# A graph network's node pass: the layer norm of the sum behind the convolution moves from VectorE to ScalarE

## The reference, cut to what matters

```python
def _layernorm(x, axis=-1, eps=1e-05):
    m = jnp.mean(x, axis=axis, keepdims=True)
    v = jnp.var(x, axis=axis, keepdims=True)
    return (x - m) / jnp.sqrt(v + eps)

h = jnp.maximum(_layernorm(x), 0.0)
x = x + _L0_gnn_ref(h, ...)    # five attention layers: h @ W, edge messages, relu
h = jnp.maximum(_layernorm(x), 0.0)
x = x + _L1_gnn_ref(h, ...)    # a * (gelu(messages) @ Wa + ba) + (1 - a) * h
h = jnp.maximum(_layernorm(x), 0.0)
x = x + _L2_gnn_ref(h, ...)    # graph convolution: gelu(norm-weighted sum of h @ W, + b)
h = jnp.maximum(_layernorm(x), 0.0)
x = x + _L3_gnn_ref(h, ...)    # out = messages + h @ W[0] + bias
```

## Time and profile before

| | |
|---|---|
| median of 3 runs | 5247.03 us (5243.42 to 5260.6) |
| profiled execution, its own time | 5250.73 us |
| its span | 5249.0 us |
| TensorE clock granted, mean | 0.882 of full speed |
| busy share PE / DVE / ACT / POOL | 81% / 77% / 63% / 61% |
| node pass, within the span | about 140 to 1567 us |

### The profile page before, as it was taken

The page is one execution under the profiler, slowest core; times in us unless marked ns, Lnnn a source line. Parts: engine busy times, 40 slices in busy tenths (PEclk is TensorE's granted clock), DMA queues, the critical chain, the costliest instruction groups (busy, mean ns, idle before and its releaser), DMA issues. The chain is left out here.

```text
span 5249.0 us, 101811 instructions
## 1 busy us (share of the span) xinstructions
PE 4269.4 (81%) x28013; PEld 3696.3 (70%) x28013; DVE 4034.0 (77%) x14947; ACT 3328.7 (63%) x9065; POOL 3228.0 (61%) x2905
## 2 busy tenths in 40 slices
PE   4899999999976978969969959877895868879575
PEld 4777777778866867858858848644775857757475
DVE  5799999999986767767757767687566968859765
ACT  2777777777755857847847848644774547768400
POOL 2888888877777727637457367222752247666277
PEclk6999999999988989989989979955997989989755
DMA  3999997666645646636636546488773759857332
GB/s 91 186 221 221 221 220 221 220 221 207 212 155 127 144 86 132 135 77 142 128 89 141 113 102 148 100 246 239 163 144 85 198 158 246 242 125 134 72 94 85
DMA packets 1107279, 825.55 MB, mean 157 GB/s; under 512 B 209510, under 2 KB 1068202, under 8 KB 1106396
## 3 DMA queue, kind: packets, MB, share of 16 engines
q1 hardware_dynamic: 1026800, 690.47, 50.7%
q0 software_dynamic: 77040, 128.08, 12.7%
q10 hardware_dynamic: 2880, 0.50, 0.1%
HBM read 374.78 MB, written 448.11 MB: 157 GB/s over the span
## 5 line engine op out<-in xcount | busy, mean ns | idle before, releaser
L806 POOL DMA_INDIRECT gat_G<-table,k_src_row x980 | 1072.8, 1095 | 316.5 <-issue 282.2
L1599 ACT ACTIVATE gat_Gw<-gat_G,gat_al 128x128 f32<-128x128 f32 x1960 | 618.5, 394 | 88.9 <-DVE gat_al L1424 88.9
L1455 DVE SCALAR_TENSOR_TENSOR gat_Gw<-gat_own,gat_al,gat_Gw 128x128 f32<-128x128 f32 x1960 | 554.7, 343 | 69.2 <-ACT gat_Gw L1599 69.0
L1716 PE MATMUL gat_psG<-gat_ends_at,gat_Gw 128*128 128x128 f32 x3920 | 538.1, 282 | 43.7 <-DVE gat_Gw L1455 43.6
L1744 PE MATMUL gat_psZ<-gat_aggT,t_gat_wh 128*128 128x256 f32 x1960 | 526.3, 392 | 15.3 <-ACT gat_hT L1625 14.9
L1716 PEld LDWEIGHTS gat_psG<-gat_ends_at,gat_Gw 128*128 128x128 f32 x3920 | 493.4, 197 | 54.9 <-DVE gat_Gw L1455 51.9
L635 PEld LDWEIGHTS nodes_psR<-t_ident_v,nodes_hTl 128*128 128x128 f32 x3168 | 431.7, 192 | 105.5 <-issue 1.8
L635 PE MATMUL nodes_psR<-t_ident_v,nodes_hTl 128*128 128x132 f32 x3168 | 446.1, 278 | 0.0
L479 POOL TENSOR_TENSOR nodes_rstd<-nodes_var,k_half 128x14 f32<-128x14 f32 x140 | 365.7, 2612 | 127.0 <-DVE nodes_var L546 127.0
L1625 ACT ACTIVATE gat_hT<-gat_psZ,t_gat_bias 128x256 f32<-128x256 f32 x490 | 231.1, 472 | 267.4 <-PE gat_psZ L1745 261.9
L1744 PEld LDWEIGHTS gat_psZ<-gat_aggT,t_gat_wh 128*128 128x128 f32 x1960 | 340.1, 194 | 56.1 <-ACT gat_aggT L1606 17.2
(11 more groups left out here) (672 smaller groups left out, 12721.8 us busy)
## 6 DMA issues: line engine op xcount, KB each, us to landing
table<-nodes_rows SPq DMA_DIRECT2D x660, 198.0 KB
table<-nodes_n SPq DMA_DIRECT2D x396, 192.0 KB
gat_own<-table SPq DMA_DIRECT2D x490, 132.0 KB
table<-gat_rows SPq DMA_DIRECT2D x392, 132.0 KB
nodes_x<-in_x SPq DMA_DIRECT2D x132, 192.0 KB
out<-nodes_x_out SPq DMA_DIRECT2D x132, 192.0 KB
gat_G<-table,k_src_row POOLq DMA_INDIRECT x980
hgt_q<-enter_q SPq DMA_DIRECT2D x98, 144.0 KB, 2.2
```

Of the source, the lines that this page charges most:

```text
L806: eng.indirect_dma_start(to, None, table, bass.IndirectOffsetOnAxis(ap=index, axis=0)).then_inc(sem, 16)
L1455: ins = eng.scalar_tensor_tensor(Gw[:, i % RS, t, h, :], own[:, i % RO, t, 0:D], al[:, g % 2, 1, a:a + 1], Gw[:, i % RS, t, h, :], ALU.mul ...
L1599: ins = eng.activation(Gw[:, i % RS, t, h, :], G[:, i % RG, t, 0:D], ACT.Copy, scale=al[:, g % 2, 0, a:a + 1])
L1716: mm = eng.matmul(o[:, h * P:(h + 1) * P], Gw[:, i % RS, t, h, :], ends_at[:, i % RE, t, :], start=True, stop=True)
```

## The change

VectorE no longer does n3. ScalarE does it, in three activations of the form Identity(rstd x input + shift), directly behind the newest block's norm and ahead of `hT6`. `shift`, which until now was only formed in steps with a newest block (k < 132), is formed in all steps that have a norm (k < 140). ScalarE signals `nC`; who waits for `nC` is as before (PE's turning of n3, SP's store, VectorE's L613). The wait for the ring of stores (`st7`) moves along with the norm.

```diff
@@ vector
                     if k < N + 8:
                         eng.wait_ge(s.small, n_small)
                         eng.wait_ge(s.pow, k + 1)
-                    if is_block(k):
+                    if k < N + 8:
                         eng.tensor_tensor(shift[:, k % 4, :], negmean[:, k % 4, :], rstd[:, k % 4, :], ALU.mult).then_inc(s.shift, 1)
...
-                    b = k - 8
-                    if is_block(b):
-                        if b >= RB:
-                            eng.wait_ge(st7[b % RB], 16 * (b // RB))
-                        normed(k, n3[:, b % RB, :, :], xs[:, b % SB, :, :], at_3, T, s.nC)
@@ scalar, behind the newest block's norm
                         ins.then_inc(s.nA, 1)
+                    d = k - 8
+                    if is_block(d):
+                        eng.wait_ge(s.shift, k + 1)
+                        if d >= RB:
+                            eng.wait_ge(st7[d % RB], 16 * (d // RB))
+                        for t in range(T):
+                            ins = eng.activation(n3[:, d % RB, t, :], xs[:, d % SB, t, :], ACT.Identity,
+                                                 bias=shift[:, k % 4, at_3 + t:at_3 + t + 1],
+                                                 scale=rstd[:, k % 4, at_3 + t:at_3 + t + 1])
+                        ins.then_inc(s.nC, 1)
                     c = k - 5
```

## The result

The changed kernel takes 5381.7 us in the median (5380.5 to 5388.3, 4 runs), the kernel before 5245.2 us (5239.1 to 5260.6, 4 runs). The ratio is 1.0263 with a 95% interval of 1.0248 to 1.0277: slower by 136.5 us, where 144 us were forecast (5391 us, range 5360 to 5450).

A forecast was written before the change was run, and what follows sets the result against it. One ScalarE-TensorE loop was taken as the bound: 142.6 us for the activations plus 1.5 us for the last steps gave 144 us, 5395 us on the profiled execution, 5391 us as median; range 5360 to 5450 us.

The forecast's parts named there:

- The size: ScalarE's half of the loop: three activations add 1.15 us in each of 124 steps, 142.6 us.
- the last steps: Last eight steps, k = 132 to 139: added shifts and the norm by ScalarE cost 1.5 us in all.
- One side sum: VectorE kept waiting at L613 could meet GpSimd's 1.02 us sum every step: 34 x 0.1 = 3 us more without slots.
- Nothing off for VectorE: Three instructions removed from VectorE, 0.77 us a step, take nothing off because no pace-setting loop goes through them.
- Rival 1: VectorE is the bound and the step shrinks by 0.77 us in 132 steps: -102 us, 5145 us; chance 0.08.
- Rival 4: Less VectorE work lets GpSimd's power, 2.6 us a step, start earlier; nothing by itself, counted to rival 2.
- rival 2: ScalarE's idle time, over 2 us a step, hides the added work and the time stays 5247 us; chance 0.06.
- The new wait closes no slower loop: VectorE's wait at L613 for n3: its loop takes 10.1 us, under the new step of 12.1 with slots.
- rival 3: VectorE's new wait at L613 closes a slower loop with stalls: 108 or 170 us more, 5499 or 5561 us; chance 0.10.
- a sign that I had named against me: Forecast wrong if steps grow by much more than 1.15 us with TensorE waiting for n2 or ScalarE for n1.
- n1's way to ScalarE: From L613 to n1's end VectorE works 7.2 us, then ScalarE 2.9 us: 10.1 us, under 12.1.
- 17 us for a clock of 0.98: TensorE's clock at 0.98 would lengthen its half by 0.14 us, 17 us over 124 steps; taken as 0, kept for the range.

The follow-up runs named there:

- experiment 1: Kernel before, VectorE keeping n3, plus three scratch activations of n3's form on ScalarE directly behind the newest block's norm: 5381.6 us, ratio 1.0271.
- experiment 2: Kernel before plus the same kind of three scratch activations, at the end of ScalarE's step: 5252.9 us beside 5244.4, ratio 1.0017.
- experiment 6: Kernel before with ScalarE's copy of the fourth layer's rows moved to the end of its step: 5249.3 beside 5259.5 us, ratio 0.9986.
- experiment 3: Changed kernel with VectorE's sum with the bias one step later, so VectorE no longer waits for n3: 5382.7 us, ratio 1.0269.
- experiment 4: Kernel before with VectorE doing n3 for one tile of three from the fourth block on: 5250.7 beside 5259.5 us, ratio 0.9988.
- experiment 9: Experiment 8 with GpSimd's sum xb put directly ahead of its power: 5221.5 us beside 5250.7, ratio 0.9949 against the kernel before.
- experiment 7: Changed kernel with n3's activations at the end of ScalarE's step and what follows n3 one step later: 5280.9 us, ratio 1.0036 against the kernel before.
- experiment 11: Kernel before with the fourth layer's row copy at the end of ScalarE's step and GpSimd's sum ahead of its power: 5248.2 us, ratio 0.9990.
- experiment 8: Experiment 7 with ScalarE's copy of the fourth layer's rows also at the end of its step: 5263.3 us, ratio 1.0009 against the kernel before.

## Why the prediction was right

*The loop.* The step was said to be ScalarE's half plus TensorE's half, closing through L754 and L793 with slots and through L797 and L709 without. After the change the ScalarE half has grown from 4.01 to 5.16 us and the TensorE half has stayed (6.94 and 6.93). Experiments 1 and 2 show it apart from everything else: the same instructions cost all or nearly nothing by place. Without slots the account was too simple. There TensorE's only wait in the step of the earlier trace rows was for L773:

```profile
1304.35 0.55 PE L627 MATMUL nodes_psA<-k_ident,nodes_rows 128*128 128x128 f32 x3 [0.19 <-ACT nodes_rows L773]
```

From there it worked on past L709; that path was as long as the one through L797. Work added ahead of both counts in full, as n3 did, but work taken off between them gives nothing, as experiment 6 shows.

*The size.* 1.15 us by L773's rows; the new activations take 1.16 and 1.15. 90 steps were to give 103.5 us and gave 99.9, since the first of them were uneven before already (two of 13.4 us by ScalarE's copies, at a clock of 0.87); 34 steps 39.1 and gave 39.9; the last steps 1.5 and gave 2.7. Sum 144.1 forecast, 140.0 in the pass with the 2.5 us less at the start, 136.5 in the medians. One side sum was off with no effect: 9.7 + 1.02 us is 0.02 us over 10.7 and not 0.1, so 1 us more without slots by the page's rule and not 3.

*Nothing off for VectorE.* Right: experiments 3 and 4. VectorE's share of 95 to 97% was in part stalls that moved nobody; it dropped by 17 points with slots and 21 without, and the kernel got slower. Rival 1 (5145 us) fails by experiment 4. The Trainium skill, "Perfetto Trace Analysis", section "Identifying the Most-Contended Engine", takes the engine with the highest occupancy as the one to optimize first, which in the steps with slots was VectorE; here the measurement decides against it. Rival 4, relief, gave nothing for this change, as forecast, but it is what experiment 9 lives on. And rival 2, that idle time hides the work, would have been right for another place, as experiment 2 shows, and not for the one chosen.

*The new wait closes no slower loop.* Right for the time (rival 3 fails: experiment 3). But half of a sign that I had named against me did show: TensorE waits for n2, 24.7 us in 45 times, against 3.9 us in 5 before. I had worked out n1's way to ScalarE and not n2's to TensorE. It is harmless because turning n2 comes in the ScalarE half: in the step above TensorE waited 0.58 us at 606.51 and then not at all for the newest block's norm, in the next it waited 0.38 us for that norm (620.13) and not for n2. It has time to give until `hT0` comes. In experiment 7, where ScalarE's half is shorter, the same kind of lateness came onto the path and cost 0.9 us a step without slots. I also took the stall to fall into VectorE's wait, at no cost; it fell on L608 or L538 and cost nothing because VectorE's round had room.

*The rule of the page.* That the loser of the shared port waits in full ("SBUF — State Buffer" of the Trainium skill, section "SBUF: two separate sides") agrees with the rows in this: VectorE's operation lasts until the sum is over (L538 at 610.95 to 611.67, the sum to 611.63) and is stretched by 0.5 to 1.4 us. But that section also says that whichever of the two starts first has the port pair. At 621.26 VectorE's operation had started 0.45 us ahead of the sum's recorded start, and it was VectorE's that took 1.89 us. By the recorded starts the measurement differs from the page there; in that step, in the one of the earlier trace rows and in experiment 7's, GpSimd was issuing an indirect DMA when the operation began and went on to the sum at once, and no run tells the two apart.

*The clock.* I had kept 17 us for a clock of 0.98 because TensorE would be less busy. It was 1.00 in both stretches after the change. So the reason I gave was wrong in its direction: TensorE was less busy, and the clock held. The 17 and 21 steps with a fall in experiments 6 and 11 all hold a wait of TensorE for n2 of 0.9 us or more, and the changed kernel's longest wait for n2 from 225 to 1225 us is 0.8 us. But such waits also go by without a fall (3 in experiment 6, 9 in experiment 11, and those of 1.1 us in experiment 7's steps without slots, at a clock of 1.00), so what decides it is not settled.

## What to carry to other kernels

Before moving work between engines, follow one step's loop: which engine waits for which, and where it closes. Work moved into the part of another engine's queue that lies on the loop costs its whole duration, even if that engine has more idle time than the work needs and the one relieved is 97% busy; behind the point where the loop leaves that engine it is nearly free (9 us in place of 136 here). A busy share can be stalls: compare an operation's mean with its shortest time (815 ns and 183 ns for L538 on 14 columns, 225 to 1225 us). And when a place is found, look again at what the shorter loop meets next; here it was another engine's stall (experiment 7), cured by moving GpSimd's sum into a wait of VectorE (experiment 9), and with slots GpSimd's round (experiments 6 and 11).

## What the runs showed of the hardware that I had not expected

- Three activations on 128 x 128 float32 with bias and scale by partition take 1.15 to 1.16 us of the queue, Identity as Relu, out of `x`, `xs` or a scratch tile.
- A VectorE operation can be stretched by a GpSimd sum of 1.0 us by more than that sum: 1.89 us for 0.56, 2.28 us for 0.86.
- TensorE's granted clock fell to half for a few microseconds at a time in some kernels of this family (0.97 and 0.96 from 200 to 1150 us in experiments 6 and 11) and not in others with more matmuls in the same time (1.00 in experiment 9). Each fall in experiments 6 and 11 stands in a step in which TensorE waits 0.9 us or more for n2; these steps together took back all that the shorter loop gave.
- GpSimd's five indirect DMA issues of a step take 5.8 and 5.9 us with n3 on VectorE and the shorter loop (experiments 6 and 11) and 5.0 and 5.1 us with n3 on ScalarE (experiments 8 and 9).
